# Attention outputs stored as four-byte numbers by head, and loaded straight into TensorE's operand buffers

## The reference, cut to what matters

```python
core = _gqa(q, k, v).reshape(b, s, nh * d)       # self attention, 16 heads of 128
xout = _gqa(qx, kx, vx).reshape(b, s, nh * d)    # attention over the context, 16 heads of 128
cat = jnp.concatenate([core, xout], axis=-1)     # 896 rows x 4096
catq = _div_clamp_fp8(cat, proj_smooth)          # clip, round to bfloat16, round to fp8 (e4m3)
return jnp.einsum('bsi,oi->bso', catq, wproj) * (proj_in_scale * proj_w_scale)
```

## Time and profile before

| | us |
|---|---|
| median of 3 runs | 2525.02 |
| lowest and highest of them | 2524.64, 2528.04 |
| span of the profiled execution | 2523.8 |

### The profile page before, as it was taken

One profiled execution on the slowest core, in us unless ns is written; L12 is line 12 of the kernel. 1 busy time (PEld: TensorE's weight loads), 2 busy tenths in 40 slices (PEclk: granted clock), 3 DMA queues, 4 the chain that ended last, 5 costly groups with the idle time before them and its releaser, 6 DMA issues. The chain is left out here.

```text
span 2523.8 us, 38343 instructions
## 1 busy us (share of the span) xinstructions
PE 2327.5 (92%) x12603; PEld 2040.6 (81%) x12603; DVE 2035.8 (81%) x3952; ACT 1089.3 (43%) x1849; POOL 944.6 (37%) x640
## 2 busy tenths in 40 slices
PE   7999999999993788869999999999999999987797
PEld 6777777779992666658999999999999999977797
DVE  8999987876766887748888888889888888881487
ACT  1000101017874666623555545555455554554332
POOL 5556100200003344433555555555565555570000
PEclk9999999999996888879999999999999999997899
DMA  9667633426634101133221222222222122106111
GB/s 388 263 259 283 221 138 147 168 91 217 224 123 155 38 30 44 44 111 104 71 71 56 72 84 84 69 83 75 84 74 72 50 81 84 61 6 176 48 52 40
DMA packets 143384, 286.66 MB, mean 114 GB/s; under 512 B 26033, under 2 KB 114178, under 8 KB 139202
## 3 DMA queue, kind: packets, MB, share of 16 engines
q1 hardware_dynamic: 137266, 265.40, 30.4%
q0 software_dynamic: 6032, 20.20, 2.2%
HBM read 203.91 MB, written 81.66 MB: 113 GB/s over the span
## 5 line engine op out<-in xcount | busy, mean ns | idle before, releaser
L1698 POOL TENSOR_TENSOR s_acc<-s_acc,s_sx 125x896 f32<-125x896 f32 x128 | 287.0, 2242 | 234.1 <-DVE s_mxh L1937 113.8
L572 DVE BATCH_NORM_STATS2 s_st<-ps 125x6 f32<-125x128 f32 x1536 | 319.2, 286 | 55.4 <-PE ps L444 48.8
L1762 ACT ACTIVATE s_sx<-s_sx 125x896 f32<-125x896 f32 x192 | 182.5, 950 | 348.5 <-DVE s_sx L1910 348.5
L1897 DVE TENSOR_TENSOR s_sx<-ps,keep_krs 125x896 f32<-125x896 f32 x192 | 209.0, 1088 | 122.7 <-PE ps L1808 119.1
L1808 PE MATMUL ps<-s_qc_hi,s_ct_hi 128*125 128x448 f32 x768 | 301.8, 393 | 1.3 <-issue 1.3
L1836 PE MATMUL ps<-s_p_hi,s_cn_hi 125*128 125x448 f32 x768 | 285.2, 371 | 2.5 <-DVE s_p_lo L1916 2.0
L1808 PE MATMUL ps<-s_qc_hi,s_ct_lo 128*125 128x448 f32 x768 | 281.9, 367 | 0.0
L1808 PE MATMUL ps<-s_qc_lo,s_ct_hi 128*125 128x448 f32 x768 | 281.8, 367 | 0.0
L1836 PE MATMUL ps<-s_p_lo,s_cn_hi 125*128 125x448 f32 x768 | 281.5, 367 | 0.0
L1836 PE MATMUL ps<-s_p_hi,s_cn_lo 125*128 125x448 f32 x768 | 281.5, 366 | 0.0
L1916 DVE TENSOR_TENSOR s_p_lo<-s_sx,s_p_hi 125x896 fp32r<-125x896 f32 x192 | 256.1, 1334 | 2.8 <-ACT s_p_hi L1767 2.8
(11 more groups left out here) (378 smaller groups left out, 5627.1 us busy)
## 6 DMA issues: line engine op xcount, KB each, us to landing
l_ahead<-in_ctxt SPq DMA_DIRECT2D x16, 1500.0 KB, 8.4
s_ct_hi<-ct_hi SPq DMA_DIRECT2D x48, 500.0 KB, 4.1
s_ct_lo<-ct_lo SPq DMA_DIRECT2D x48, 500.0 KB, 4.8
s_cn_raw<-in_ctx SPq DMA_DIRECT2D x48, 500.0 KB
l_raw<-in_ctxt SPq DMA_DIRECT2D x15, 1500.0 KB, 10.5
l_raw<-in_w SPq DMA_DIRECT2D x16, 1024.0 KB, 5.3
ct_hi<-l_hi SPq DMA_DIRECT2D x8, 1500.0 KB, 12.5
ct_lo<-l_lo SPq DMA_DIRECT2D x8, 1500.0 KB, 16.0
```

Of the source, the lines that this page charges most:

```text
L572: ins = dve.bn_stats(st[:, G * t + g, :], kx[0:TT, t % NB, g // 4, DH * (g % 4):DH * (g % 4) + DH])
L1698: pool.tensor_tensor(a, a, p[:, PR * w.pt:PR * w.pt + PR, :], ALU.add).then_inc(s["acc_ready"], 1)
L1762: act.activation(p, p, ACT.Exp).then_inc(s["exp_ready"], 1)
L1897: dve.tensor_tensor(by_group(sx[w.h][:, tiles, :]), by_group(sc[st % 2]), krs_b[:, tiles, HG * w.h:HG * w.h + HG].unsqueeze(3).to_broadcas ...
```

## The change

- The DRAM tensor `io.cat` was [16 sequences, 128, 32 heads x 56] in bfloat16. It becomes [128, 32 heads, 896 rows] in float32.
- `cats` and `cat` of the two attention stages become float32. A pair's store in self attention becomes one DMA for both sequences, 896 KB, whose pieces in DRAM are 448 bytes long (112 rows of one head): 16 pieces for each of 128 partitions. A unit's store in cross attention is 224 KB, in pieces of 224 bytes (56 rows of one head): 8 for each partition.
- In the projection the buffer `cat[r]` and ACT's conversion go. The DMA writes `catr[r]`, 14336 contiguous bytes for each partition on both sides, 1792 KB. SP waits for `products` at c-1, the end of the matmuls of chunk c-2, ahead of both loads. PE waits for `loaded[r]` where it waited for `cat_ready`.

```diff
@@ self_attention
-        cats = m.sb("cats", [P, 2, NH, S], BF16)
+        cats = m.sb("cats", [P, NH, PAIR])
                 def store_cat(q):
                     sp.wait_ge(s["cat_ready"], NQ * (q + 1))
-                    for b in range(2):
-                        sp.dma_start(io.cat[bass.ds(2 * q + b, 1), :, 0:NH * S].rearrange("b p n -> p (b n)"),
-                                     cats[:, b, :, :].rearrange("p h s -> p (h s)")).then_inc(s["cat_stored"], 16)
+                    sp.dma_start(io.cat[:, 0:NH, bass.ds(PAIR * q, PAIR)], cats[:, :, :]).then_inc(s["cat_stored"], 16)
-                sp.wait_ge(s["cat_stored"], 32 * NP)
+                sp.wait_ge(s["cat_stored"], 16 * NP)
-                        pool.wait_ge(s["cat_stored"], 32 * q)
+                        pool.wait_ge(s["cat_stored"], 16 * q)
-                    hb = lambda x: x[:, :, :].rearrange("p h (b s) -> p b h s", b=2)
-                    pool.tensor_tensor(cats[:, :, QC * a:QC * a + QC, :], hb(cs), hb(cc), ALU.subtract).then_inc(s["cat_ready"], 1)
+                    pool.tensor_tensor(cats[:, QC * a:QC * a + QC, :], cs[:, :, :], cc[:, :, :], ALU.subtract).then_inc(s["cat_ready"], 1)
@@ cross_attention
-        cb, ce, cc, cat = [m.sb(n, [P, QH], BF16) for n in ("cb", "ce", "cc", "cat")]
+        cb, ce, cc = [m.sb(n, [P, QH], BF16) for n in ("cb", "ce", "cc")]
+        cat = m.sb("cat", [P, QH])
-                    at = (NH + h * NH // 2) * S
-                    sp.dma_start(io.cat[bass.ds(b, 1), :, at:at + NH // 2 * S].rearrange("b p n -> p (b n)"), cat[:, :]).then_inc(s["cat_stored"], 16)
+                    at = NH + h * NH // 2
+                    sp.dma_start(io.cat[:, at:at + NH // 2, bass.ds(S * b, S)], by_head(cat[:, :])).then_inc(s["cat_stored"], 16)
@@ layer1_projection
-        cat = [m.sb(f"cat{r}", [P, B, HC, S], BF16) for r in range(2)]
-        catr = [m.sb(f"catr{r}", [P, HC, B, S], F32R) for r in range(2)]
+        catr = [m.sb(f"catr{r}", [P, HC, N], F32R) for r in range(2)]
                         if not first(i):
-                            sp.wait_ge(s["cat_ready"], c - 1)
-                            sp.wait_ge(s["w_lo_ready"], c - 1)
-                        sp.dma_start(cat[r][:, :, :, :].rearrange("p b h s -> p b (h s)"), io.cat[:, :, bass.ds(c * HC * S, HC * S)]
-                                     .rearrange("b p n -> p b n")).then_inc(loaded[r], 16)
+                            sp.wait_ge(s["products"], c - 1)
+                        sp.dma_start(catr[r][:, :, :].bitcast(F32), io.cat[:, bass.ds(c * HC, HC), :]).then_inc(loaded[r], 16)
                         act.activation(w_hi[r][:, :, :], w[r][:, :, :], ACT.Copy).then_inc(s["w_hi_ready"], 1)
-                        for h in range(HC):
-                            ins = act.activation(catr[r][:, h, :, :], cat[r][:, :, h, :], ACT.Copy)
-                        ins.then_inc(s["cat_ready"], 1)
-                        pe.wait_ge(s["cat_ready"], c + 1)
+                        pe.wait_ge(loaded[r], 32 * i + 32)
                         pe.wait_ge(s["w_lo_ready"], c + 1)
-                                    mm = pe.matmul(acc[:, t, :], catr[r][:, h, 2 * t:2 * t + 2, :], x[r][:, h, :],
+                                    mm = pe.matmul(acc[:, t, :], catr[r][:, h, PAIR * t:PAIR * t + PAIR], x[r][:, h, :],
@@ program
-        io.cat = nc.dram_tensor("cat", [B, P, 2 * NH * S], BF16, kind=KIND_DRAM).ap()
+        io.cat = nc.dram_tensor("cat", [P, 2 * NH, N], F32, kind=KIND_DRAM).ap()
```

More of the change, by code:

```diff
@@ L1966, in layer1_projection @@
         loaded = [m.sem(f"loaded{r}") for r in range(2)]
-        s = {k: m.sem(k) for k in ("x_loaded", "cat_ready", "w_hi_ready", "w_lo_ready", "products", "dve_steps")}
+        s = {k: m.sem(k) for k in ("x_loaded", "w_hi_ready", "w_lo_ready", "products", "dve_steps")}
         acc = ps[0:PAIR, 0:4, :].rearrange("p b (u n) -> p (b u) n", n=D)
```

## The result

| | before | after |
|---|---|---|
| median of 4 runs, us | 2524.83 | 2544.69 |
| lowest to highest | 2523.54 to 2528.04 | 2544.43 to 2549.80 |
| span of the profiled execution | 2523.8 | 2543.2 |

The changed kernel takes 1.0080 times as long, with a 95% interval of 1.0064 to 1.0095: slower by 0.8%, 19.9 us by the medians. The forecast was 2542.5 us.

What follows compares the result with a forecast made beforehand. TensorE, busy 92% of the span, was taken to bound the kernel and set the projection's pace. 10.2 + 3.5 - 0.8 + 3.1 + 1.5 = +17.5 us on 2523.8 gives 2541.3, plus 1.2 for the median: 2542.5 us, range 2531 to 2554.

Steps and rivals of the forecast that it cites:

- The likeliest case: Whole kernel: slower, 2542.5 us, mainly from TensorE pauses in the projection; own range 2533 to 2552, chance 0.73.
- The loads start later: Projection: loads wait for chunk c-2's matmuls, so TensorE pauses 3.4 us ahead of chunks 2, 4, 6; +10.2 us.
- The loads grow: Projection: a chunk's load grows to 2304 KB and lands in 8.3 us instead of 7.1; bounds 7.1 and 9.5.
- The clock: Projection: two of three pauses are followed by half clock on TensorE; +3.5 us (0 to 5.3).
- The start: Projection's start: landing grows 1.2 us, conversion's 2.0 us go; -0.8 us (-2.0 to +0.4).
- The stores: Last stores ending the attention stages take longer: self attention +3.1 us, cross attention +1.5 us.
- Half pace for small writes: Rival, attention-end stores: small-piece writes take twice as long beyond 1.5 us fixed; 6 us more, 2548.5; chance 0.15.
- Cross attention and POOL's writes: Cross attention's other 31 stores have room, and POOL's four-byte writes add 0, under 0.3 us either way.
- The rival on the other side: Projection: loads land within 4.9 us of issue, so TensorE never pauses; 2524.6 us, not slower; chance 0.07.

Runs made afterwards that it cites:

- wait_only: The kernel before, with only the loads of chunk c made to wait for the matmuls of chunk c-2; 2546.4 us, 1.0087 of before.
- staged: The changed kernel with staging buffers back, now float32: loads go to cat[r] and ACT converts to catr[r]; 2531.5 us, 1.0027 of before.
- ring4: The changed kernel with four operand and weight buffers instead of two, the eight chunks written out; 2527.6 us, 1.0013 of before.
- w_early: The changed kernel with each chunk's weights loaded first, on their own semaphore, not waiting for chunk c-2's matmuls; 2527.1 us, 1.0013 of before.
- filler: The changed kernel with ten more matmuls, results unused, ahead of chunks 2, 4 and 6; 2540.3 us, 1.0062 of before.
- unrolled2: The changed kernel with the projection's eight chunks written out in place of the loop, still two buffers; one execution, 2549.1 us.
- before_halves: The kernel before, keeping its stores and conversions, with sixteen two-head chunks, four buffers, weights first, written out; 2520.1 us, 0.9977 of before.
- halves: The changed kernel with sixteen two-head chunks, four buffers, weights first, and a store per quarter pair in self attention; 2519.7 us, 0.9982 of before.

## Why the prediction was right

The likeliest case came true: slower, 2544.7 against 2542.5, by the mechanism that it named. The projection grew by 17.1 us, where the sum had 12.9. Step by step:

- *The loads start later*: right, and shown by wait_only alone; staged, ring4 and w_early each take the pauses away or nearly so. 12.7 us were measured for 10.2, as the pauses were 4.8, 4.6 and 3.3 instead of 3.4 each. The reasoning fits the third. In the first two the landing took 1.4 us longer, with an instruction packet among its packets, which the step didn't have. No pause came ahead of chunks 3, 5 and 7, as said.
- *The loads grow*: right for a load without such a packet, 8.2 us for chunk 6 and 8.4 for chunk 0, where 8.3 were taken; chunks 2 and 4 had 9.7 and 9.6, above the bound of 9.5. The row of the large loads gave the 8.3. In staged the growth costs the stage's start 0.9 us and no pause. The fit that the Trainium skill gives, "DMA: Bandwidth & Descriptors", section "Anatomy of one DMA — SWDGE (gpsimd) path", made it 7.4 us. It is a fit for DMAs issued from GpSimd, and these are issued by SP; the measured 8.2 decides here.
- *The clock*: right in kind. What the stage grew by beyond pauses and start is 17.1 - 12.7 + 0.9 = 5.3 us for 3.5; filler gives 4.5 back. Chunk 2 took 1.5 us and chunk 4 2.6 us longer than a chunk at full clock, 4.1 in all; the rest is spread in parts of half a us and less. Two pauses of three were followed by half clock, as taken, but after the second it lasted 5.6 us or more. That the third was not is close to luck: in unrolled2, with a packet in its load, it was 4.4 us, and the clock fell there too.
- *The start*: right, 2292.37 - 2281.41 = 10.96 us, -0.9 for -0.8. The landing grew by 1.1 us for 1.2, and the 2.0 us of conversion went.
- *The stores*: right in kind, too dear: +2.2 for +3.1 and +0.7 for +1.5, because a store landed in 5.1 us or less, not in the cat load's 5.5, and the one of cross attention in 2.4, not 3.2. Half pace for small writes is refuted by 5.1 us; the read-modify-write that the Trainium skill, "DMA: Bandwidth & Descriptors", section "Specifications", has below 512 bytes does not show as a doubled landing, though short pieces do cost 1.5 us more than long ones.
- *Cross attention and POOL's writes* at nothing: nearly. The kernels with the by-head store have 1163.1 to 1164.4 us there, those without 1162.4 to 1162.9; some 1 us that I did not count. By the times of the stage's own stores, 0.2 to 0.5 us of it is there when the first of them is issued, so they can't be the cause of that part (before_halves, with the stores of before, is 0.3 us off the other way). What causes it isn't shown.
- *The rival on the other side* (loads hidden) needed a landing within 4.9 us; it was 8.4. w_early came near it by another way, making less hang on the landing instead of making it quicker.

The terms that were too small (4.3 us of pauses and clock) and too large (1.7 us of stores) partly cancel, so the 2.2 us between forecast and measurement flatter the sum.

## What to carry to other kernels

A staging buffer and its copy can look like waste, since the copy lies beside other work, and yet be what lets the next load start early. Before it is taken out, write down for each buffer which event frees it, and compare the time from that event to "operand ready" (landing and everything chained behind it) with the work that is left in the other buffers: here 10.8 to 12.3 us against 7.5. If it doesn't fit, more and smaller buffers in the same memory (halves) or taking the small operand off the chain (w_early) repair it. In these runs each of the unfilled pauses of 4.0 to 5.5 us ahead of a chunk was followed by half clock, and those of 3.3 us and less were not.

## What the runs showed that I had not expected

- One 16 KB packet of the instruction queue, some 0.9 to 1.2 us on one of 16 DMA engines, goes with a landing some 1.4 us later of a load that all 16 share (ten loads with it, five without; a matching, not a proof).
- Half clock after a pause of 4.6 us cost 2.6 us at chunk 4, where the pause in the earlier trace rows had cost 1.75.
- The start of a stage was worth more than its steady part: 6.6 us in halves, and 5.0 in before_halves, from half-sized chunks and weights first, with no byte less moved.
- For the same 896 KB, 448-byte pieces landed 1.5 us later than 7168-byte pieces (5.1 against 3.6).
